# An agent-attention layer, causal attention and a mixture of experts on one core: the experts by sorted blocks of rows, the maxima as rows of the stack, the first layer in batches

## The reference

```python
# layer 1, on the group-normalized x: attention to 16 learned agents, SiLU MLP, and back
out  = mlp(attn(q(x), k(agents), v(agents), pe1)) + x          # 8 heads of 16
fin  = mlp(attn(q(agents), k(out), v(out), pe2))               # 16 rows, repeated 4 x 4
x    = x + fin_upsampled + out + gn(x)
# layer 2, on the layer-normalized tokens: causal attention, 8 heads of 16, 256 tokens
t    = t + softmax(q k^T / 4, causal) v @ W_out + b_out + ln(t)
# layer 3, on the layer-normalized tokens: experts
probs   = softmax(ln(t) @ W_router)                            # 8 experts
combine = the two largest, scaled to sum 1, zero elsewhere
t    = t + sum over e of combine[e] * (relu(ln(t) @ W1[e] + b1[e]) @ W2[e] + b2[e])
```

## Time and profile before

| what | us |
|---|---|
| median of three runs | 423.76 (423.04 to 423.99) |
| span of the profiled execution | 421.5 |
| own time of the profiled execution | not given apart from its span |
| TensorE busy in it | 389.2 |
| VectorE, ScalarE, GpSimd busy | 242.0, 223.1, 143.2 |
| first expert matmul starts | at 83.8 |

### The profile page before, as it was taken

The page is one execution under the profiler, slowest core; times in us unless marked ns, Lnnn a source line. Parts: engine busy times, 40 slices in busy tenths (PEclk is TensorE's granted clock), DMA queues, the critical chain, the costliest instruction groups (busy, mean ns, idle before and its releaser), DMA issues.

```text
span 421.5 us, 10143 instructions
## 1 busy us (share of the span) xinstructions
PE 389.2 (92%) x3382; PEld 375.8 (89%) x3382; DVE 242.0 (57%) x822; ACT 223.1 (53%) x698; POOL 143.2 (34%) x198
## 2 busy tenths in 40 slices
PE   0867788799999999999999999999999999999997
PEld 0756678599999999999999999999999999999997
DVE  3445754686369737774578637873687366323321
ACT  1023354177455764496348644774567645665442
POOL 2137200374025521463037303740255115700640
PEclk9989999799999999999999999999999999999999
DMA  7920010020001100020002000200011000200000
GB/s 255 342 81 2 21 37 2 0 45 16 1 2 34 37 2 2 19 50 0 0 9 59 0 0 0 47 22 0 0 34 34 0 0 22 50 0 2 14 0 14
DMA packets 15305, 13.24 MB, mean 31 GB/s; under 512 B 3376, under 2 KB 12848, under 8 KB 15280
## 3 DMA queue, kind: packets, MB, share of 16 engines
q1 hardware_dynamic: 14416, 12.15, 10.6%
q10 hardware_dynamic: 864, 0.76, 0.6%
HBM read 7.13 MB, written 1.05 MB: 19 GB/s over the span
## 4 chain that ended last, share of the span: by engine, by line
PE 76%; DVE 15%; issue 3%; DMA 2%; ACT 1%; SPq 1%; POOL 1%; DVEq 1%; ACTq 0%; POOLq 0%
PE bY L803 19%; PE bH L781 6%; PE bH L783 6%; PE bH L782 6%; PE bS L803 5%; PE bA L759 3%; PE bA L758 3%; PE bH L817 2%; PE bS L726 2%; PE bA L757 2%; PE bT L703 2%; PE bT L705 1%; PE bT L704 1%; DMA x_all<-xT 1%; PE bL L644 1%
## 5 line engine op out<-in xcount | busy, mean ns | idle before, releaser
L564 ACT ACTIVATE hf<-bH,b1s 128x256 f32<-128x256 f32 x256 | 101.2, 479 | 41.8 <-PE bH L783 41.8
L803 PE MATMUL bY<-w2s,hf 128*128 128x128 f32 x768 | 96.4, 276 | 0.0
L803 PEld LDWEIGHTS bY<-w2s,hf 128*128 128x128 f32 x768 | 90.7, 192 | 0.0
L781 PE MATMUL bH<-xhi,w1hi 128*128 128x256 f32 x256 | 78.3, 306 | 0.2 <-ACT hf L564 0.2
L783 PE MATMUL bH<-xhi,w1lo 128*128 128x256 f32 x256 | 72.3, 282 | 0.0
L782 PE MATMUL bH<-xlo,w1hi 128*128 128x256 f32 x256 | 72.0, 281 | 0.0
L1168 DVE SCALAR_TENSOR_TENSOR acc<-bY,comb,acc 128x128 f32<-128x128 f32 x80 | 24.3, 345 | 53.0 <-PE bY L803 53.0
L781 PEld LDWEIGHTS bH<-xhi,w1hi 128*128 128x128 f32 x256 | 48.9, 191 | 1.4 <-ACT hf L564 0.4
L782 PEld LDWEIGHTS bH<-xlo,w1hi 128*128 128x128 f32 x256 | 49.0, 191 | 0.2
L783 PEld LDWEIGHTS bH<-xhi,w1lo 128*128 128x128 f32 x256 | 48.4, 189 | 0.0
L430 POOL TENSOR_TENSOR bw<-b2r,comb 128x256 f32<-128x256 f32 x64 | 40.9, 638 | 21.8 <-DVE comb L1151 15.9
(11 more groups left out here) (183 smaller groups left out, 806.9 us busy)
## 6 DMA issues: line engine op xcount, KB each, us to landing
stack<-split SPq DMA_DIRECT2D x144, 32.0 KB, 2.0
w1raw<-w SPq DMA_DIRECT2D x8, 256.0 KB, 6.9
w2s<-w SPq DMA_DIRECT2D x8, 256.0 KB, 6.7
x_all<-xT SPq DMA_DIRECT2D x2, 512.0 KB, 5.3
out<-ob SPq DMA_DIRECT2D x8, 128.0 KB, 1.8
W<-weights SPq DMA_DIRECT2D x1, 512.0 KB, 7.6
b2r<-b ACTq DMA_DIRECT2D x1, 512.0 KB, 9.0
W<-weights SPq DMA_DIRECT2D x1, 384.0 KB, 7.1
```

Of the source, the lines that this page charges most:

```text
L564: act.activation(hf[:, e % 2, k, :], bH[k // 2][:, (k % 2) * TOK:(k % 2 + 1) * TOK], ACT.Relu, bias=b1s[:, e, k:k + 1]).then_inc(mo_r.sem, 1)
L781: pe.matmul(hk, w1hi[:, e, wk], xhi[:, :], start=True, stop=False)
L803: mm = pe.matmul(y_bank(e)[:, t * P:(t + 1) * P], hf[:, e % 2, k, t * P:(t + 1) * P], w2s[:, e, k, :], start=(k == 0), stop=(k == HB - 1))
```

## The change

The kernel is written anew from the first layer to the output.

*Experts.* The normalized row of each token is scattered twice, with the number of its destination as a 129th column, to the DRAM tensor `rows_in`, in which each expert has a region of 2048 rows. The positions come from counts: a matmul with a triangle of ones over the one-hot picks (`cum`). The tensor is filled with zeros first. After images 3, 5 and 7 VectorE works out a table (`table`, some 22 dependent small operations): for the blocks 0 to 8, 9 to 16 and 17 to 38 the expert and the first row. A block loads 128 rows and its expert's W1 with bias by numbers read from the table (`value_load`), and computes transpose (`X`), first layer (`H`) and second layer (`Y`) in fp32; POOL scatters its result by row number to `rows_out`. After all 39 blocks both results of each token are loaded back, weighted and summed. The split of W1 and the bias sums on GpSimd go.

*Attention.* All eight heads use the stack, filled by three transfers for an image. Scores are computed once for the maxima (`S0` to `S5`, units of four heads or two). The negated maxima are transposed, split into two parts, and written by two transfers (`mr`) as rows 48 and 49 of the stack, against rows of ones. Scores are then computed again turned, keys on partitions (`E0` to `E5`), with the maxima subtracted in the same matmul; ACT takes 512 exponentials at a time, which are already the stationary operand for the values (`V0` to `V7`); a column of ones in the values gives the sums.

*First layer.* It goes by batches of 1, 1, 2, 2 and 2 images, each operation on the whole batch; SiLU is a tanh and a product. Parts of the work move between engines: normalizing to ACT, the low parts of the split to DVE.

*Order.* The slots are replaced by ticks, with offsets by engine (`LATER`, not shown). The loop is written out. Spare matmuls are 10 in each tick before 48, and 48 in each attention frame (`W0` to `W7`).

```diff
+BATCHES = ((0, 1), (1, 2), (2, 4), (4, 6), (6, 8))
...
-LOW = 80.0
+K_DOT = STACKED * DK
...
+S_UNITS = (("row0", 0), ("row1", 0), ("row1", 2), ("row0", 4), ("row1", 4), ("row1", 6))
+E_UNITS = (("col1", 0), ("col0", 0), ("col0", 2), ("col1", 4), ("col0", 4), ("col0", 6))
+UNITS = 6
+S_RING = UNITS + 1
...
+REGION = TOKENS
+SPAN_BLOCKS = REGION // P
+TABLES = {3: (0, 9), 5: (9, 17), 7: (17, 39)}
+BLOCKS = 39
...
+ROWS_OUT = 4
+W_RING = 6
+W_ROW = HID + HB
+CHUNK = 4
...
+FRAME = 16
+FIRST = 48
+L0_STAGES = {
+    "xg": 0, "s1": 1, "p1": 3, "pt": 4, "z": 6, "zs": 7, "o": 8, "s2": 10, "v": 10, "p2": 12, "qt": 14,
+    "f": 15, "y": 17, "ys": 18, "w": 19, "x1": 21, "ln": 23, "xl": 24, "lt": 25, "q": 26, "k": 28, "va": 30}
+AT_STAGES = {
+    "st": -16, "S0": -13, "S1": -12, "S2": -12, "S3": -10, "S4": -9, "S5": -8, "mt": -6, "mr": -4, "E0": 0,
+    "E1": 1, "E2": 3, "E3": 5, "E4": 7, "E5": 9, "V0": 3, "V1": 4, "V2": 6, "V3": 7, "V4": 10, "V5": 11,
+    "V6": 12, "V7": 13, "W0": 2, "W1": 5, "W2": 6, "W3": 10, "W4": 8, "W5": 9, "W6": 11, "W7": 12, "on": 13,
+    "ot": 14, "wo": 17, "n2": 19, "nt": 20, "lg": 22, "cum": 25, "tab": 27}
+L0_BEGIN = (
+    0, 4, 32, 66, 98)
+MO_BEGIN = (
+    129, 133, 138, 142, 147, 151, 154, 159, 164, 167, 170, 172, 175, 177, 185, 186, 191, 194, 196, 199, 201,
+    203, 206, 207, 209, 210, 213, 215, 217, 220, 221, 223, 225, 227, 229, 231, 233, 236, 238)
+MO_STAGES = {
+    "load": -12, "X": 0, "H": 3, "Y": 6}
...
+            sp.wait_ge(su_zero, 1)
+            sp.dma_start(rows_in.rearrange("(p r) c -> p (r c)", p=P).rearrange("p (z n) -> p z n", z=ZEROS),
+                         zero.unsqueeze(1).broadcast_to([P, ZEROS, EXPERTS * REGION * ROW // P // ZEROS]))\
+              .then_inc(su_rows, 16)
...
+                if what == "st":
...
+                    for n, (q, k) in enumerate(((QHI, KHI), (QLO, KHI), (QHI, KLO))):
+                        sp.dma_start(stack[n * DK:(n + 1) * DK, i % 2, :, :, :].bitcast(F32),
+                                     split[:, q:k + 1:k - q, own].bitcast(F32))\
+                          .then_inc(at_stack[i % 2].sem, 16)
...
+                if what == "load":
+                    i, n = begin(b)
+                    if n == 0:
+                        sp.wait_ge(tb_ready, 1 + list(TABLES).index(i))
+                        sp.wait_ge(rt_sent[i], SENT_N[i])
+                    row_no = sp.value_load(tab_r[i][0:1, n:n + 1], min_val=0, max_val=EXPERTS * REGION - P)
+                    if b >= ROWS_IN:
+                        sp.wait_ge(mo_out.of(b - ROWS_IN), mo_out.done(b - ROWS_IN))
+                    sp.dma_start(xb[:, b % ROWS_IN, :], rows_in[bass.ds(row_no, P), :]).then_inc(mo_in.of(b), 16)
+                    e = expert(sp, b)
+                    if b >= W_RING:
+                        sp.wait_ge(mo_r.sem, mo_r.nth(b - W_RING))
+                    sp.dma_start(w1b[:, b % W_RING, :], w1[bass.ds(e, 1), :, :].rearrange("a p n -> (a p) n"))\
+                      .then_inc(mo_w.of(b), 16)
...
+                if what == "mr":
...
+                    for n in range(2):
+                        act.dma_start(stack[K_DOT + n:K_DOT + n + 1, i % 2, :, 0, :].bitcast(F32), mT[0:HEADS, n, :].bitcast(F32))\
...
+                    act.activation(to, bE[u % 2][:, :], ACT.Exp).then_inc(at_e.sem, 1)
...
+                    if kind == "col1":
+                        for q in range(h, h + 4):
+                            pe.matmul(bank[:, (q - h) * P:(q - h + 1) * P], stack[0:K_ALL, two, q, 1, P:TOK],
+                                      stack[0:K_ALL, two, q, 0, P:TOK], start=(q == h), stop=False)
+                        pe.matmul(bank[:, :].rearrange("p (h n) -> p h n", n=P), causalb,
+                                  identb.unsqueeze(1).broadcast_to([P, 4, P]), start=False, stop=True)\
+                          .then_inc(at_c.sem, 1)
+                    else:
+                        for q in range(h, h + 2):
+                            pe.matmul(bank[:, (q - h) * TOK:(q - h + 1) * TOK], stack[0:K_ALL, two, q, 1, 0:P],
+                                      stack[0:K_ALL, two, q, 0, :], start=(q == h), stop=False)
+                        pe.matmul(bank[:, :].rearrange("p (h n) -> p h n", n=TOK)[:, :, 0:P], causalb,
+                                  identb.unsqueeze(1).broadcast_to([P, 2, P]), start=False, stop=True)\
...
+                    outs = [bA[:, (t * HEADS + h) * (DK + 1):(t * HEADS + h + 1) * (DK + 1)] for t in range(TILES)]
+                    pe.matmul(outs[0], ec0[:, h, 0:P], v[:, max(g, 1) % 2, first, h, :], start=True, stop=True)
+                    pe.matmul(outs[1], ec0[:, h, P:TOK], v[:, max(g, 1) % 2, first, h, :], start=True, stop=False)
+                    pe.matmul(outs[1], ec1[:, h, :], v[:, max(g, 1) % 2, first + 1, h, :], start=False, stop=True)\
...
+                if what[0] == "W":
+                    for _ in range(WARM_AT):
+                        pe.matmul(bA[:, 3 * P:4 * P], identb, causalb, start=True, stop=True)
...
+                    for t in range(TILES):
+                        for k in range(PICKS):
+                            pool.indirect_dma_start(
+                                out=rows_in, out_offset=bass.IndirectOffsetOnAxis(ap=slot[:, i, k, t:t + 1], axis=0),
+                                in_=lnx[:, i * TILES + t, k, :], in_offset=None, bounds_check=EXPERTS * REGION - 1,
+                                oob_is_err=False).then_inc(rt_sent[SENT[i]], 16)
...
+                    goes_to = goes[:, b:b + 1] if TABLE_OF[b] == LAST else xb[:, b % ROWS_IN, C:C + 1].bitcast(U32)
+                    pool.wait_ge(mo_yb.sem, mo_yb.nth(b))
+                    pool.indirect_dma_start(
+                        out=rows_out, out_offset=bass.IndirectOffsetOnAxis(ap=goes_to, axis=0),
+                        in_=y[:, b % ROWS_OUT, :], in_offset=None, bounds_check=PICKS * TOKENS - 1,
+                        oob_is_err=False).then_inc(mo_out.of(b), 16)
...
+                    pe.transpose(x_bank, xb[:, b % ROWS_IN, 0:C], ident).then_inc(mo_x.sem, 1)
...
                     for k in range(HB):
+                        mm = pe.matmul(h_bank[:, k * P:(k + 1) * P], w1b[:, b % W_RING, k * P:(k + 1) * P], xbT[:, two, :],
+                                       start=True, stop=True)
...
+                    e = expert(pe, b)
...
+                    for k in range(HB):
+                        mm = pe.matmul(y_bank, hT[:, two, k, :],
+                                       w2s[:, bass.ds(e, 1), k, :].rearrange("p a c -> p (a c)"),
                                        start=(k == 0), stop=(k == HB - 1))
...
+            for c in range(IMAGES * TILES // CHUNK):
+                dve.wait_ge(co_in[c], 16 * PICKS)
+                for t in range(c * CHUNK, (c + 1) * CHUNK):
+                    dve.scalar_tensor_tensor(out=t2[:, t, :], in0=back[:, t, 0, :], scalar=tw[:, t, 0:1], in1=t2[:, t, :],
+                                             op0=ALU.mult, op1=ALU.add).then_inc(co_one.sem, 1)
+                for t in range(c * CHUNK, (c + 1) * CHUNK):
+                    dve.wait_ge(co_one.sem, co_one.nth(t))
+                    dve.scalar_tensor_tensor(out=t2[:, t, :], in0=back[:, t, 1, :], scalar=tw[:, t, 1:2], in1=t2[:, t, :],
+                                             op0=ALU.mult, op1=ALU.add).then_inc(co_acc.sem, 1)
```

More of the change, by code:

```diff
@@ L83, in before, with __init__, of, done @@
         return i * self.per
-def first(i):
-    return isinstance(i, int) and i == 0
-def hybrid_block(nc, xT, consts, weights, cols, rows, agents, w_router, w1, b1, w2, b2, out):
+class Ring:
+    def __init__(self, ctx, nc, name, size):
+        self.sems = [ctx.enter_context(nc.semaphore(f"{name}{n}")) for n in range(size)]
+        self.size = size
+    def of(self, b):
+        return self.sems[b % self.size]
+    def done(self, b):
+        return 16 * (b // self.size + 1)
+    def total(self, n, count):
+        return 16 * len(range(n, count, self.size))
@@ L92, in hybrid_block @@
+def hybrid_block(nc, xT, consts, weights, cols, rows, agents, w_router, w1, w2, b2, rows_in, rows_out, out):
     ctx = ExitStack()
@@ L182, in hybrid_block @@
[L182 to L191, removed]
+        zh = sb("zh", [P, 1])
+        half_w = sb("half_w", [P, 2, P])
+        wq_s = sb("wq_s", [P, P])
+        bq_s = sb("bq_s", [P, 1])
+        xg = sb("xg", [P, WTOK])
@@ L232, in tiles @@
+        bS = [ctx.enter_context(nc.psum_tensor(f"bS{n}", [P, 4 * P], F32)) for n in range(2)]
+        bE = [ctx.enter_context(nc.psum_tensor(f"bE{n}", [P, 4 * P], F32)) for n in range(2)]
         def tiles(ap):
@@ L314, in _ @@
+        SENT = {}
+        for i in range(IMAGES):
+            SENT[i] = min(n for n in TABLES if n >= i)
+        SENT_N = {n: 16 * PICKS * TILES * sum(1 for i in range(IMAGES) if SENT[i] == n) for n in TABLES}
         @block.sync
@@ new lines, in _ @@
+            ticks = Ticks("sp")
+            for tick in range(TICKS):
```

(13 more changed lines are left out.)

1668 lines of the change are left out of this document (873 added, 795 removed).

## The result

The changed kernel takes 473.5 us (median of four runs, 466.6 to 490.2) where the kernel before, on the same chip, takes 423.9: 1.104 times as long, interval 1.090 to 1.117. The forecast was 342, range 308 to 385. The profiled execution has a span of 464.7 us, 124.7 more than the sum.

The account below looks back on a forecast made before the run. TensorE was taken to set the pace. 57 us to image 0's exponentials, 187 of frames, 23 for image 7's tail, 53 for 22 blocks, 4 drain and 16 combine gave 340 of span; plus 2.2, 342 us, range 308 to 385.

Parts of the forecast that it names:

- 24: two engines near each other and a batch chain with gaps: Steady attention frames: TensorE and VectorE loads close together, plus batch-chain gaps, add about 6%, giving 24 us a frame.
- the floor of 22: Attention frames: TensorE's own work asks for at least 22 us a frame, 24 with blocks among it.
- 3.0 us for eight heads: Attention scores: 3.0 us an image before; computing them twice was to cost 5.4 to 6.0 us.
- Rival D: The 22 blocks standing alone run at 1.2 GHz, 3.82 us each, 31 us more: 373 us; chance 0.07.
- 3.5 us: Head, after image 0's queries are split: the transfers to the stack take 3.5 us.
- a full cover for the maxima: Between scores and exponentials: about 4 us for the maxima's way, hidden by the neighbour image's work.
- image 0 at 57: Head: image 0's exponentials come at 57 us, after queries split at 43.5, transfers, score units and maxima.
- 9.5 for a lone image: Head, image 0 without cover: score units alternating with reductions 5 us, then the maxima's way 4.5.
- The block count and the price of a block: Experts: at most 39 blocks of 128 rows, 1.91 us each on TensorE; the last 22 stand alone.
- The 0.5 for a register load: Expert blocks: loading the expert number into a register takes 0.5 us on TensorE for each block.
- C: Rival on the 71 indirect scatters: from 3.2 us each POOL sets the pace; at 3.7, 378 us; chance 0.15.
- F: Rival on the same scatters: from 4.3 us each the kernel is slower than before; chance 0.08.

Follow-up runs that it names:

- e10: Changed kernel with both score matmuls over 128 rows, result kept, batches 2 to 4 six ticks earlier, 5 spares a tick before tick 48 instead of 10: 404.7 us.
- e13: Kernel before the change, with its six stacked heads scored over the 48 rows holding data in place of 128: 452.1 us (1.065).
- e17: e10 with three of each attention group's six spare matmuls over 48 rows, alternating with those over 128: 483.5 us (1.138).
- e18: e10 with the first three of each attention group's six spare matmuls over 48 rows, the last three over 128: 433.0 us (1.017).
- e3: Changed kernel with only the second score matmuls over all 128 rows, the added rows zero: 442.2 us (1.044).
- e4: Changed kernel with both score matmuls over all 128 rows, using stale maxima and scaled exponential input, so other output: 405.8 us (0.958).
- e11: Changed kernel with its narrow scores kept and only batches 2 to 4 of the first layer begun six ticks earlier: 480.1 us (1.130).
- e1: Changed kernel without its 48 spare matmuls in each attention frame: 479.7 us (1.133).
- e9: Changed kernel with full-row scores, result kept, and earlier batches; 16 KB of zeros replaces each 256 KB stack transfer from image 2 on, other output: 393.1 us (0.925).
- e14: As e10, but with no spare matmuls before tick 48: 405.8 us (0.958).
- e16: e10 with the first score matmuls over 64 rows, the second over 128: 434.6 us.

## Why the prediction was wrong

**The step that failed** is the frame length, "24: two engines near each other and a batch chain with gaps", on the floor of 22. It measured 38.0, and seven frames are 98 of the 124.7 us missed.

*The scores.* The prediction took 3.0 us for eight heads from the earlier trace rows and doubled it. The section on the kernel before speaks of a matmul of 48 rows; 48 hold data, but the matmuls of the earlier trace rows contract all 128 rows of the stack, and the change cuts them to 48 and 50. I never asked whether the rows in use change the price. They do: at full clock a four-head unit is 0.91 us in the kernel after and 0.40 + 0.23 = 0.63 in e10's chain, one of two heads 0.64 and 0.36. That is 0.28 a unit, 3.4 a frame. Over 128 rows, as in e10, the twelve units are 4 x 0.63 + 8 x 0.36 = 5.4 us: the price taken was right for the matmul that it was read from. e13 has the cost in the kernel before, e17 and e18 by itself.

*The clock.* The larger part. A frame has 24 changes of the row count (into and out of twelve units), and the granted clock over the frames is 0.64; with half of the changes gone (e3) it is 0.75, with all of these gone (e4) 0.85. That it is the changes and not the narrow rows is shown with the spares of e17 and e18, and for the scores it is inferred from there. Everything else on TensorE's queue is longer too. 243.27 busy us at 0.64 are some 156 at full clock, 22 a frame (an estimate). So the 38.0 us are about 22 of work, 12.5 that the low clock adds (88 of the 98 us) and 3.3 in which TensorE idles. That 22 is the floor of the prediction is partly luck: it has the 3.4 of the changes in it, which the prediction hadn't, so its other terms were 2 to 3 us too high; e10, without changes, comes to 165.73 x 0.85 / 7 = 20.

Rival D had the clock, with 0.07, but in the 22 blocks, where it is 0.99. (Its sum also leaves out the 0.5 us that the main sum has in each block; with it, 384 in place of 373.) The reason given for it, a wait before the fall, isn't needed: the fall at 89.5 us has none, and e11 gained nothing by starting the batches earlier. The argument for a high clock, "busy in four fifths of that stretch", held in that stretch and is no rule: e1's frames are busy for 92% at 0.52. A full record is no full rate. (Trainium skill, TensorE: Matmul & The Clock Gate, A second HAM failure mode: psum-queue depth-cycling: very short pauses between groups of matmuls can make the clock swing. By that rule a record without visible waits can lose its clock; the fall at 89.5 us agrees, the 20 us at a steady 0.50 don't look like a swing, and no record here shows the pauses themselves.)

*Transfers.* "3.5 us" for the stack and a full cover for the maxima were too low. The 256 KB transfers land after 6.0 us in the median and 8.0 at most; the maxima's stand there with 7 where the large ones are on the way. TensorE idles 22.9 us of the frames, 15.0 of them until a transfer to the stack landed. e9 prices the large ones at 2.0 us a frame.

*What is left.* e10's frames are 28.8. Of the 4.8 over 24, e9 explains 2.0. The rest goes with a clock that is still 0.85 and with waits; whether the order alone could bring the frames to 24, no run tells.

**The head**: "image 0 at 57", measured 83.7. The queries and keys were split at 51.4, not 43.5: in the chain from 14 to 62 the tick's spare matmuls, ten at a time, are 21.7%. Then:

```profile
17.80 2.15 PE bA L989 x20
...
52.85 7.69 DMA stack<-split
60.59 0.66 PE bS L842 x4
```
So 8 of the 27 us were lost before the split. From there to the landing of the stack it is 9.1 us with the two issues ahead of it, where "3.5" stood: 5.5 more. From 60.6 to 82.7 the first image's units stand between matmuls of the batch behind it, whose own chain of small steps has to pass, and between more spares; to the first exponential it is 23 us where I had 9.5 for a lone image, 13.5 more. What the spares cost there is open: with none of them (e14) the head isn't shorter, but its clock is at 0.61.

**What was right.** The block count and the price of a block: 22 blocks, drain and combine 73.2 against 73, a block 54.2 / 22 = 2.46 us against 2.41. Its matmuls are the 1.91 forecast (0.11 + 0.89 + 0.91 in the chain). The 0.5 for a register load isn't shown as such: the load is 0.30 + 0.15 us on TensorE's load queue, but TensorE's waits in these blocks are for the rows' load (3.6 us in all) and VectorE (1.7). The scatters, which rivals C and F needed at 3.2 and 4.3 us, are at 0.97 to 0.99 on POOL in the mean and 1.18 at most (I took 1.2); groups by line of the kernel after:

```profile
L577 POOL DMA_INDIRECT rows_in<-lnx,slot x32 | 31.5, 985 | 111.0 <-DVE slot L1274 103.6
L586 POOL DMA_INDIRECT rows_out<-y,goes x22 | 21.3, 967 | 27.9 <-DVE y L1355 26.0
```
The zero fill landed in 26.5 us (I took 21) and delayed nothing. So F gave the right sign and the wrong cause: slower than before, though not by a scatter.

**Open.** e13 has 24 changes of the row count in a frame of 47 us, as many as the kernel after in 38. Its clock falls to 0.54 in the stretch before the first expert matmul and stays at 1.00 in the frames that have expert work between the changes. What in the company of the changes decides whether the clock falls is not settled, nor why a change costs 0.10 us among spares and 0.13 to 0.14 around scores.

## What to carry to other kernels

Before reusing a matmul's duration, see that the rows in use stay the same: here it was cheaper to contract over 128 rows, most of them zero, than over 48 between matmuls of 128. Read the granted clock by window before trusting busy time; a queue that is full to the last microsecond can run at half rate. Where narrow matmuls can't be avoided, put them together, since the price is paid at each change.

## What the runs showed of the hardware

- A change between 48-row and 128-row matmuls holds TensorE's queue for 0.10 us at full clock and 0.11 at the lower level in a group of spares (e17), and for 0.13 to 0.14 around scores (e13, kernel after against e10); in e17 and e18 as much again goes with a lower clock. Scores over 64 rows cost the same 0.91 and 0.64 us a unit as over 48 (e16).
- The clock fell to 0.50 in a stretch in which TensorE's record has no gap (84 to 92 us), and stood at 0.50 for 20 us in another. Contracting the scores over some 80 more rows, all zero, took 64 us off the kernel's time (e4).
- An indirect scatter of 128 rows took 0.97 to 0.99 us on POOL in the mean and landed after 2.5 (`rows_in`) and 2.9 us (`rows_out`) in the median.
